# Prologue of a low-rank-adapter and recurrence kernel: loads, TensorE program and layout of x's first rows rearranged

## What is computed

```python
mu = mean(ada_emb); var = mean(square(ada_emb - mu))
c = (ada_emb - mu) / sqrt(var + 1e-5) * ln_gamma + ln_beta
h = gelu(c @ W1 + bias1)
w = h @ W2 + bias2                       # (B, 4 * D * R)
a1, b1, a2, b2 = [t.reshape(B, D, R) for t in split(w, 4)]
u = einsum('btd,bdr->btr', x, a2)
mid = gelu(x @ base_down + einsum('btr,blr->btl', u, b2))
v = einsum('blr,btl->btr', b1, mid)
x = x + (x + mid @ base_up.T + einsum('bkr,btr->btk', a1, v))
# second layer, a recurrence over t that starts from cond
next_h = tanh(x[:, t] @ Wx + b + prev_h @ Wh)
out = x + hs
```

## Time and profile before

| | us |
|---|---|
| median of 3 runs (lowest to highest) | 526.85 (526.58 to 527.3) |
| the profiled execution's own time | 527.65 |
| its span | 525.9 |
| PE busy | 505.6 (96%) |
| DVE busy | 291.8 (55%) |
| ACT busy | 175.2 (33%) |
| POOL busy | 22.2 (4%) |
| DMA queue of SP, share of 16 engines' span | 7.8% |

### The profile page before, as it was taken

How to read it: one execution, slowest core, us unless ns; L and a number is a source line. 1 busy time by engine, 2 the same in 40 slices (tenths; PEclk the granted TensorE clock), 3 DMA queues, 4 the chain that set the end, 5 groups by cost and what they waited for, 6 DMA issues and landing times.

```text
span 525.9 us, 33134 instructions
## 1 busy us (share of the span) xinstructions
PE 505.6 (96%) x14756; PEld 471.9 (90%) x14756; DVE 291.8 (55%) x2272; ACT 175.2 (33%) x1158; POOL 22.2 (4%) x35
## 2 busy tenths in 40 slices
PE   9999999999999999999999999999999999998885
PEld 6569999999999999999999999999999999998884
DVE  2535565565556556555655555555655655565553
ACT  3103333333333333333333333333333333333322
POOL 7350000000000000000000000000000000000000
PEclk9999999999999999999999999999999999999999
DMA  8970000000000000000000000000000000000000
GB/s 292 401 213 4 4 14 4 4 14 4 14 5 14 6 7 11 4 14 4 15 4 14 4 6 14 4 14 4 14 4 5 14 4 15 4 14 3 14 6 11
DMA packets 8114, 16.05 MB, mean 31 GB/s; under 512 B 500, under 2 KB 5924, under 8 KB 7972
## 3 DMA queue, kind: packets, MB, share of 16 engines
q1 hardware_dynamic: 7904, 13.90, 7.8%
q10 hardware_dynamic: 68, 0.05, 0.0%
HBM read 11.85 MB, written 2.10 MB: 27 GB/s over the span
## 4 chain that ended last, share of the span: by engine, by line
PE 94%; ACT 3%; issue 1%; DVE 1%; DVEq 0%; POOL 0%; POOLq 0%
PE bank L881 64%; PE bank L801 7%; PE bank L845 4%; PE bank L826 3%; ACT h_ring L462 3%; PE bank L850 2%; PE bank L840 2%; PE bank L821 2%; PE bank L831 2%; PE bank L648 2%; PE bank L682 2%; PE bank L810 1%; PE bank L661 1%; PE bank L785 1%; PE bank L869 1%
## 5 line engine op out<-in xcount | busy, mean ns | idle before, releaser
L881 PE MATMUL bank<-h_ring,whp 128*128 128x52 bf16 x6132 | 243.3, 186 | 13.2 <-ACT h_ring L462 13.2
L544 DVE TENSOR_TENSOR r_ring<-h_ring 128x4 f32<-128x4 f32 x1022 | 136.6, 164 | 205.7 <-ACT h_ring L462 203.2
L462 ACT ACTIVATE h_ring<-bank 128x4 f32<-128x4 f32 x1024 | 142.1, 174 | 320.3 <-PE bank L881 312.5
L881 PE MATMUL bank<-r_ring,whp 128*128 128x52 bf16 x4096 | 220.5, 185 | 0.0
L881 PEld LDWEIGHTS bank<-h_ring,whp 128*128 128x128 bf16 x6132 | 187.9, 96 | 34.2 <-ACT h_ring L462 25.8
L881 PEld LDWEIGHTS bank<-r_ring,whp 128*128 128x128 bf16 x4096 | 174.6, 96 | 0.0
L881 PE MATMUL bank<-l_ring,whp 128*128 128x52 bf16 (+1 forms) x2048 | 157.4, 178 | 0.0
L548 DVE TENSOR_TENSOR l_ring<-r_ring 128x4 bf16<-128x4 f32 x1024 | 136.2, 162 | 0.0
L881 PEld LDWEIGHTS bank<-l_ring,whp 128*128 128x128 bf16 x2048 | 122.5, 96 | 0.0
L801 PE MATMUL bank<-xp,wxp 128*128 128x32 bf16 x1488 | 63.0, 176 | 0.0
L801 PEld LDWEIGHTS bank<-xp,wxp 128*128 128x128 bf16 x1488 | 50.5, 96 | 0.0
(11 more groups left out here) (123 smaller groups left out, 240.4 us busy)
## 6 DMA issues: line engine op xcount, KB each, us to landing
w_sb<-in_L_cond_W SPq DMA_DIRECT2D x16, 512.0 KB, 11.5
out<-o_sb SPq DMA_DIRECT2D x16, 128.0 KB
x_sb<-in_x SPq DMA_DIRECT2D x3, 512.0 KB, 15.2
x_sb<-in_x SPq DMA_DIRECT2D x2, 256.0 KB, 9.6
w_sb<-in_L_cond_W SPq DMA_DIRECT2D x1, 256.0 KB, 3.6
down_sb<-in_L_cond_base_down SPq DMA_DIRECT2D x1, 256.0 KB, 5.0
wh_sb<-in_L_cond_Wh SPq DMA_DIRECT2D x1, 256.0 KB, 11.1
up_sb<-in_L_cond_base_up SPq DMA_DIRECT2D x1, 256.0 KB, 11.3
```

Source lines behind the costliest of these rows:

```text
L462: nc.scalar.activation(h_ring[:, m, slot(pair, s), 0:B], zt, ACT.Tanh).then_inc(h_ready, 1)
L544: nc.vector.tensor_tensor(r_ring[:, k, q, 0:B], state_before(pair, s, k)[:, 0:B], state_hi_before(pair, s, k)[:, 0:B], ALU.subtract).then_ ...
L881: return nc.tensor.matmul(zbank(p, q, m)[:, col0:col0 + n], whp[part][:, k, P * m:P * (m + 1)], rhs[:, 0:n], start=False, stop=stop, skip_ ...
```

## The change

Loads. SP's queue was: x's first 64 rows, W1, base_down, A2, B2, Wh, base_up, B1, Wx, A1, x's rows 64 to 127, the rest of x. It is now: W1, base_down, Wh, A2, x's first rows, B2, base_up, Wx, B1, A1, x's rows 64 to 127, the rest. W1 is read as two neighbouring rows to a partition (`(p k) n`, 2 KB runs in place of 1 KB), and cn is turned with the matching stride. x's first 128 rows go to two tiles `xa_sb` and `xb_sb` of 128 partitions x 2 rows, so that a batch takes 32 partitions; their transposes are 128 x 128, and ACT writes `xT` with every second column (stride 2). On ACT's queue bias2 is issued ahead of b; cond, gamma, beta and bias1 stand there as before.

PSUM. B1 and A1 lie in the right halves of the banks of A2 and B2 (before, in the same halves), so that their bias products can run early.

TensorE, all in another order, with `w_products` cut into halves in three places. ACT makes the gelu ahead of the copies to `xT`.

```diff
-            sp.dma_start(x_sb[0:T0, :, 0], x[:, 0:T0].rearrange("b p d -> p b d")).then_inc(ld_x[0], 16)
-            sp.dma_start(w1_sb[:], W1.rearrange("(k p) n -> p k n", p=P)).then_inc(ld_w1, 16)
+            sp.dma_start(w1_sb[:], W1.rearrange("(p k) n -> p k n", p=P)).then_inc(ld_w1, 16)
             sp.dma_start(down_sb[:], base_down.rearrange("(k p) n -> p k n", p=P)).then_inc(ld_down, 16)
+            sp.dma_start(wh_sb[:], Wh.rearrange("(k p) n -> p k n", p=P)).then_inc(ld_wh, 16)
             load_w2(A2)
+            sp.dma_start(xa_sb[:].rearrange("p r d -> p (r d)"),
+                         x[:, 0:T0].rearrange("b (q r) d -> b q (r d)", r=2)).then_inc(ld_xa, 16)
             load_w2(B2)
-            sp.dma_start(wh_sb[:], Wh.rearrange("(k p) n -> p k n", p=P)).then_inc(ld_wh, 16)
             sp.dma_start(up_sb[:], base_up.rearrange("(k p) n -> p k n", p=P)).then_inc(ld_up, 16)
+            sp.dma_start(wx_sb[:], Wx.rearrange("(k p) n -> p k n", p=P)).then_inc(ld_wx, 16)
             load_w2(B1)
-            sp.dma_start(wx_sb[:], Wx.rearrange("(k p) n -> p k n", p=P)).then_inc(ld_wx, 16)
             load_w2(A1)
...
-        PLACE = {A2: 0, B2: 2, B1: 0, A1: 2}
+        PLACE = {A2: (0, 0), B2: (2, 0), B1: (0, HC), A1: (2, HC)}
...
             for k in range(K2):
+                act.wait_ge(tr_ready, k + 1)
+                nc.scalar.copy(xT[:, k, :, 0:T0].rearrange("p b (q r) -> p r b q", r=2),
+                               bank[6 + k][:, 0:B * T0].rearrange("p (r b q) -> p r b q", r=2, b=B)).then_inc(tr_moved, 1)
...
             def first_transposes(k):
-                for b in range(B):
-                    last = nc.tensor.transpose(bank[6 - k][:, T0 * b:T0 * (b + 1)], x_sb[0:T0, b, 0, P * k:P * (k + 1)],
-                                               ident[0:T0, 0:T0])
+                for r in range(2):
+                    last = nc.tensor.transpose(bank[6 + k][:, P * r:P * (r + 1)], xa_sb[:, r, P * k:P * (k + 1)],
+                                               ident[:])
...
+            keep_busy(10)
+            pe.wait_ge(ld_bias2, 16)
+            pe.wait_ge(quadrant_ready, 1)
+            bias_product(A2, 0)
+            pe.wait_ge(cn_ready, 1)
...
+            bias_product(B2, 1)
             for c in range(2):
-                bias_product(A2, c)
+                bias_product(B1, c)
             pe.wait_ge(grep_ready, 1)
             w_products(A2, 0)
-            bias_product(B2, 0)
-            w_products(A2, 1)
-            bias_product(B2, 1)
-            keep_busy(4, 7)
-            w_products(B2, 0)
-            pe.wait_ge(fac_ready[A2], 2)
-            turn_factor(A2, a2T_psum)
-            for c in range(2):
-                bias_product(B1, c)
+            w_half_products(A2, 1, 0)
+            bias_product(A1, 0)
+            w_half_products(A2, 1, 1)
+            pe.wait_ge(ld_xa, 16)
+            first_transposes(0)
+            first_transposes(1)
+            bias_product(A1, 1)
...
```

More of the change, by code:

```diff
@@ L144, in adaptive_lowrank_then_recurrence @@
         ld_bias2 = sem("ld_bias2")
-        ld_x = [sem(f"ld_x{n}") for n in range(NTT)]
-        ld_x_more = sem("ld_x_more")
+        ld_xa = sem("ld_xa")
+        ld_xb = sem("ld_xb")
+        ld_x = [sem(f"ld_x{n}") for n in range(1, NTT)]
         ld_down = sem("ld_down")
@@ L676, in base_down_product, with w_half_products @@
                                  start=(k == 0), stop=False, skip_group_check=True)
+            def w_half_products(j, c, k):
+                pe.wait_ge(ld_w2[j][c][k], 16)
+                for e in range(NCH):
+                    last = nc.tensor.matmul(wbank(j, c)[Q * e:Q * (e + 1), :], gRep[:, k].rearrange("p b r -> p (b r)"),
+                                            w2_sb[:, k, j, HC * (NCH * c + e):HC * (NCH * c + e + 1)], start=False,
+                                            stop=(k == K2 - 1), skip_group_check=True)
+                if k == K2 - 1:
+                    last.then_inc(w_ready[j], 1)
             def w_products(j, c):
                 for k in range(K2):
-                    pe.wait_ge(ld_w2[j][c][k], 16)
-                    for e in range(NCH):
-                        last = nc.tensor.matmul(wbank(j, c)[Q * e:Q * (e + 1), :],
-                                                gRep[:, k].rearrange("p b r -> p (b r)"),
-                                                w2_sb[:, k, j, HC * (NCH * c + e):HC * (NCH * c + e + 1)], start=False,
-                                                stop=(k == K2 - 1), skip_group_check=True)
-                last.then_inc(w_ready[j], 1)
+                    w_half_products(j, c, k)
             def turn_factor(j, done):
@@ L709, in a1_first_product @@
                                  stop=True, skip_group_check=True).then_inc(up_psum, 1)
-            pe.wait_ge(ld_x[0], 16)
-            first_transposes(0)
-            first_transposes(1)
-            keep_busy(4)
+            keep_busy(10)
[3 more added lines that the diff above has]
+            pe.wait_ge(cn_ready, 1)
+            for k in range(K2):
+                last = nc.tensor.transpose(bank[5][:, D + B * k:D + B * (k + 1)], cn[:].rearrange("b (p k) -> b k p", k=K2)[:, k],
+                                           ident[0:B, 0:B])
+            last.then_inc(cT_psum, 1)
+            bias_product(A2, 1)
+            bias_product(B2, 0)
             pe.wait_ge(ld_bias1, 16)
@@ L769, in _ @@
                 keep_busy(4, 6)
-            w_products(B1, 0)
-            for c in range(2):
-                bias_product(A1, c)
             pe.wait_ge(upT_ready, 1)
@@ L919, in recurrence @@
                             first_input_product(0, m, 1).then_inc(z_ready, 1)
[L920 to L923 removed]
+                        for m in range(K2):
+                            first_input_product(1, m, 1)
                     if TURN <= s < TURN + K2 and not first:
```

94 lines of the change are left out of this document (46 added, 48 removed).

## The result

| | before | after |
|---|---|---|
| median (lowest to highest), 6 runs each | 526.86 (526.25 to 527.45) | 532.83 (528.54 to 535.9) |
| ratio, 95% interval | | 1.0109 [1.0066, 1.0152] |
| profiled execution, its span | 527.65, 525.9 | 532.43, 530.6 |
| mean granted clock, profiled execution | 0.999 | 0.986 |
| mean granted clock, the six runs | | 0.980 to 0.991 |

The account below looks back on a forecast made before the run. TensorE's own stream (94% of the span) was taken as the bound: 1.56 us gained up to the recurrence and 0.3 in it, 1.86, less 0.25 for cuts, gave 1.6 less, 526.85 to 525.25 us, range 523.9 to 527.2.

Parts of the forecast that it names:

- The new stream: The changed program priced place by place, prologue into recurrence: 1.86 us gained, less 0.25 for cuts.
- Prices: TensorE unit costs from before's trace: a filler 0.224 us at the start, 0.109 later; a bias product 0.53.
- the rule on the clock: TensorE: a PE that idles is throttled to half rate again, so a long stop brings the 0.224 us filler back.
- slower case: First bias product behind the ten fillers waits for bias2; measurably slower if it lands from 9.5 us; chance 0.12.
- Steps 1 and 2: Start to W1: ten fillers for twelve, bias2 taken at 6.83, W1 done at 9.86, gRep costs no wait.
- Steps 3 and 4: A2's products to the end of B2: A2 done at 14.07, B2 at 20.53, 0.86 us gained.
- Step 4: x's transposes to the end of B2: done at 20.53 against 21.39 before, 0.86 us gained.
- step 3: A2's products end at 14.07; x's first rows land at about 12.9, 1.2 us before PE asks.
- Step 5: Behind B2: b2d ready at 21.76, PE asks at 22.41, so the standing goes; place passed at 23.3, before 24.26.
- the rule on the shared port: DVE with two SBUF inputs and POOL reading SBUF exclude each other; a late second b2d costs up to 0.5 us.
- Steps 6 to 8: Turning of B1 to first input product, k = 1: turning from 28.55, that row at 36.3 against 37.57, gain 1.56 us.
- Step 9: Recurrence: two steps with 128 x 128 transposes last 0.94 in place of 1.08 each, 0.3 us together.

Follow-up runs that it names:

- b_late: Kernel before with its four base_down products moved behind the turning of A2; 530.26 us against 527.37, ratio 1.0047.
- b_thin: Kernel before with all 56 fillers behind the first 16 made 4 rows deep in place of 128; 535.19 us against 527.07, ratio 1.0169.
- b_tail: Kernel before with only the change's last part: A1's second part in halves, a bias and input product ahead, fewer fillers there; 526.58 us, ratio 0.9987.
- b_best: b_tail_xb without the four fillers ahead of the first B2 products; 525.24 us against 526.97 for before, ratio 0.9971.
- b_tail_xb: b_tail with x's rows 64 to 127 on 128 partitions, in four loads; 526.36 us, ratio 0.9987 against before.
- experiment 2: Changed kernel with x's first rows, and rows 64 to 127, loaded by four DMAs each, one to a batch; 532.97 us against 527.33, ratio 1.0096.
- a_clock: Changed kernel with nine fillers put early, B1's bias products behind base_up and nine fillers at B1 gone; 530.3 us against 527.33, ratio 1.0073.
- a_both: Changed kernel with the edits of a_clock and of experiment 2; 530.35 us over twelve runs against 527.33, ratio 1.0042 over nine.
- a_dense: Changed kernel, x's loads split in four, twelve fillers in place of six early bias products, B1's eighteen fillers gone; 532.75 us against 527.37, ratio 1.0104.
- a_strong: Changed kernel, x's loads split, 64 fillers in eights around early thin products, nine at B1 gone; 531.93, 532.93, 541.82, 544.25 us.
- a_wide: Changed kernel, x's loads split, every bias product made 128 rows deep with zeros, DVE clearing the tile first; 534.03 us, ratio 1.0113.
- b_late_fill: b_late with 16 fillers where the four base_down products had stood; 528.9 us against 526.97, ratio 1.0037.

## Why the prediction was wrong

**The step that failed** is a price used through all of "The new stream": that a product costs behind the first twelve fillers what it costs in the trace of before, the upper clock being taken as reached for good. It was written down in two places: "0.109 later" under Prices, and, after the rule on the clock, "In my sum PE nowhere stands longer than 0.1 us before 32 us, so it belongs to the slower case alone". I tied the clock to PE's standing. The runs showed in its place 13.65 us at 1.2 GHz, from 10.27 to 23.92, with PE 100% busy, and so a B2 finished 6.99 us late. They tie the clock to what PE does as well: at 100% busy it fell in after, in b_late and in b_thin. The Trainium skill ("TensorE: Matmul & The Clock Gate", Part 1) has the gate go by how busy PE has been of late; read with "busy" as the profile's busy share, the trace contradicts it (13.60 of 13.60 us busy at 0.50), and b_thin shows that the rows in use have a part in it.

By steps:

- **Steps 1 and 2** had sizes right: W1 ended 0.24 late. The fillers took 2.17 and not 1.84, since the clock first rose at 6.86 and in before at 6.17. The prediction took this for a price of the program, and it is one of the execution: the twelve fillers took 2.06 us in before, 1.42 in b_tail and b_best, 2.41 in b_tail_xb. bias2 had landed at 6.42 in this execution (6.83 forecast) and PE did not wait. In five of the experiments bias2 came at 5.9 to 7.6 where nothing held back its issue, and PE stood 0.33 to 1.53 us for it. So the slower rival's wait exists, in part because PE is early, but it is not what made the profiled execution of after slow.
- **Steps 3 and 4** carry the loss. Step 4 even counted the cause as a gain: "Fourteen fillers have left this stretch (1.5), and two bias products came in (1.06)". The trade was of thick for thin work, and 13.6 us at half clock was its price: 6.8 us if all of it would have run twice as fast, and 6.75 is what the stretch from W1 to the end of B2 took beyond the forecast (17.42 for 10.67).
- **The load in step 3** was mis-sized as well: 12.9 forecast for x's first rows, 16.6 measured, for the reason of experiment 2. With the clock held, PE would have asked at 14.07 and stood 2.5 us, which is more than the whole forecast gain: by step 3's own reckoning the kernel as built would have come out near 527.8, 0.9 above before and outside the range. This is an estimate; no run has this load at full clock. The slow clock hid it, and a_clock stood 1.57.
- **Step 5**: b2d no longer ends a wait; it took 0.55 and 0.29. All came 7 us later, so the 0.5 us that the rule on the shared port might have cost could not show here. The rule itself the traces bear out. In the profiled executions b2d took more than 0.29 us twelve times, from 0.35 to 1.21, and each time a subtraction or a cast of POOL was under way when it started, and b2d ended 0.14 to 0.15 us behind POOL's instruction. b_tail, POOL and the second b2d:

```profile
21.20 1.15 POOL L365 TENSOR_TENSOR wres<-wres,whp 128x512 f32<-128x512 f32 x1
```

```profile
21.30 1.21 DVE L531 TENSOR_TENSOR b2d<-fac,qmask 128x128 f32<-128x128 f32 x1
```

  PE stood behind this b2d: B2 to L767 took 2.20 us in b_tail and 1.74 in before, the 0.5 that the prediction had feared.
- **Steps 6 to 8** held: 15.88 us from the end of B2 to the first input product, 15.77 forecast.
- **Step 9** held. PE's timeline of after, the starts of three steps with a transpose pair between them:

```profile
47.19 0.48 PE L890 MATMUL bank<-h_ring,whp 128*128 128x52 bf16 x12
...
48.13 0.48 PE L890 MATMUL bank<-h_ring,whp 128*128 128x52 bf16 x12
...
49.08 0.48 PE L890 MATMUL bank<-h_ring,whp 128*128 128x52 bf16 x12
```

0.94 and 0.95, where a step took 1.08.

**How much of the sum was right.** The lengths of PE's own work were, wherever the clock was up: steps 1 and 2 within 0.24, steps 6 to 8 within 0.11, step 9. Steps 3 and 4 no run of the changed kernel shows at full clock. If what the lower level costs, (1 - clock) x span, is taken off each run's span, the median is 524.2 for before (73 executions) and 522.8 for after (six), 1.4 us less where 1.6 was forecast. This is a rough estimate: it takes all the time at the lower level as PE's, it leaves out a late first rise, and of b_thin's four executions it makes 522 three times and 529 once. That it meets the forecast is in part luck, since PE came to x's rows too late to stand for them. The two fast executions of a_both point the same way, but their order has nine fillers moved and x's load split, so they do not show the sum of the kernel as built.

**The chances.** My slower case had 0.12 and hung on bias2. A case "the thinner stretch loses the clock" was to be had from the rows of before: the fillers stood among the thin products, and the profile of before showed the clock move only once, when the fillers had run. I priced their removal at their own length, though a filler is there for the clock and for nothing else.

**What stays open.** Why a_dense and a_strong fell at all: the wait for bias2 of 0.6 us, the thin share behind it, or both. Whether bias products made 128 rows deep would hold the clock; a_wide was to tell and could not. What W1's products, with their four columns, have to do with it: no run changes them alone. The price of the four-engine load at full clock. Why A2's last load comes 1.5 us later with four small loads behind it. Why one program falls in some executions and not in others.

## What to carry to other kernels

Before a filler or a thick product is taken out or traded, read the granted clock of that stretch and look at which products would be left in it, full ones or ones of a few rows, and not only at PE's busy share; "PE never stands" does not mean that its clock is safe. Price a kernel that has come near this edge by a dozen runs with their clocks, not by one profile, for its time is then a spread of 7 to 9 us. And look at the outermost dimension of each load's pattern: here four batches there went with four landings in place of sixteen, and everything queued behind came 2 to 4 us late. Compare single executions only from the first rise of the clock on, for the same fillers ahead of it differed by 1 us between executions.

## What the hardware did that I had not expected

- TensorE dropped to 1.2 GHz with no idle time: 6.70 of 6.70 us busy at 0.50 in b_late, the same at 1.00 in b_late_fill with 16 thick fillers more.
- Fillers with 4 rows in place of 128 cost 8 us (535.19 against 527.07) and did not hold the clock.
- The same twelve fillers at the start took 1.42, 2.06 or 2.41 us, as the clock first rose at 3.83 or 4.35, 6.17 or 6.90.
- A DVE operation of 0.29 us took up to 1.21 when it started while POOL was in a subtraction or a cast, and ended 0.14 to 0.15 us behind it, in twelve cases of twelve.
- The fall varies from execution to execution of one program: a_both's mean clock went from 0.983 to 0.997 and its time from 534.96 to 525.72.
- A 256-KB load on 4 engines brought the mean pace of all loads from 403 to 265 GB/s over 4.3 us, and B2's four loads 3.6 to 4.2 us later than before.
- A wait of 0.6 us for bias2 stood ahead of a fall of the clock at 10.32 (a_dense) and at 13.9 (a_strong), so thick work after a stop does not always save it; whether the stop has a part in the fall is open.
